# Idle waits of TensorE taken out, and steps around them reordered, in a fused attention kernel

## What is computed

```python
def _cross_attention(q_in, kv_in, wq, bq, wk, bk, wv, bv, wo, bo, bias_k, bias_v):
    qh = (q_in @ wq + bq).reshape(b, q_len, H, K)          # H = 16 heads, K = 128
    kh = (kv_in @ wk + bk).reshape(b, t, H, K)             # and one more key: bias_k
    vh = (kv_in @ wv + bv).reshape(b, t, H, K)             # and one more value: bias_v
    logits = jnp.einsum('bqhk,bthk->bhqt', qh, kh) / scale
    weights = jax.nn.softmax(logits, axis=-1)
    ctx = jnp.einsum('bhqt,bthk->bqhk', weights, vh).reshape(b, q_len, H * K)
    return ctx @ wo + bo
x = x + _cross_attention(_layer_norm(x, ...), ctx_2048, ...)   # first attention
x = x + _cross_attention(_layer_norm(x, ...), ctx_2048, ...)   # second attention
x = x + gelu(_layer_norm(x, ...) @ w_fc1 + b_fc1) @ w_fc2 + b_fc2
```

## Time and profile before

| | |
|---|---|
| median of 3 runs | 1567.48 us (1567.3 to 1568.53) |
| profiled execution | 1566.88 us |
| its span, first to last instruction | 1565.1 us |
| PE busy | 96% of the span |
| DVE, ACT, POOL busy | 62%, 56%, 27% |
| granted clock of TensorE | 0.997 on average |
| first block, to the end of the second's scores | 0 to 72.8 us |
| turn and block after | 455.5 to 538.9 us |
| last four steps | 867 to 922 us |

### The profile page before, as it was taken

One profiled execution on the slowest core, in us unless ns is written; L12 is line 12 of the kernel. 1 busy time (PEld: TensorE's weight loads), 2 busy tenths in 40 slices (PEclk: granted clock), 3 DMA queues, 4 the chain that ended last, 5 costly groups with the idle time before them and its releaser, 6 DMA issues. The chain is left out here.

```text
span 1565.1 us, 41346 instructions
## 1 busy us (share of the span) xinstructions
PE 1500.6 (96%) x17264; PEld 1301.6 (83%) x17264; DVE 970.8 (62%) x2122; ACT 874.0 (56%) x1638; POOL 419.4 (27%) x449
## 2 busy tenths in 40 slices
PE   4999999999999799999999999999999999999996
PEld 4788888888897688888888888988878988888864
DVE  4765646555467655564656676479996658865366
ACT  3835354363455453454453366577777567775476
POOL 1431020220201510210210123036774206542052
PEclk9999999999999999999999999999999999999998
DMA  5101010010010010010010000020002000001001
GB/s 173 42 29 42 1 68 2 28 43 1 28 42 1 28 42 2 28 43 1 29 42 29 28 2 28 1 83 3 3 29 82 1 16 15 30 2 28 8 22 54
DMA packets 17832, 46.20 MB, mean 30 GB/s; under 512 B 1360, under 2 KB 11616, under 8 KB 14704
## 3 DMA queue, kind: packets, MB, share of 16 engines
q1 hardware_dynamic: 13456, 39.33, 7.3%
q10 hardware_dynamic: 4192, 4.24, 0.8%
HBM read 39.37 MB, written 4.19 MB: 28 GB/s over the span
## 5 line engine op out<-in xcount | busy, mean ns | idle before, releaser
L174 PE MATMUL ps<-ch,W 128*128 128x512 f32 (+1 forms) x2484 | 579.4, 383 | 2.5 <-DVE ch L602 1.2
L174 PEld LDWEIGHTS ps<-ch,W 128*128 128x128 f32 x2484 | 435.6, 188 | 86.9 <-issue 3.8
L174 PEld LDWEIGHTS ps<-W,split_arena 128*128 128x128 f32 x3084 | 388.4, 188 | 23.1 <-issue 4.8
L174 PE MATMUL ps<-W,split_arena 128*128 128x256 f32 x3084 | 401.9, 283 | 3.1 <-DVE split_arena L1726 2.3
L1221 ACT ACTIVATE arena<-ps,hbias 128x512 f32<-128x512 f32 x128 | 87.8, 689 | 213.1 <-PE ps L174 195.2
L174 PE MATMUL ps<-W,ch 128*128 128x512 f32 (+1 forms) x864 | 195.2, 382 | 6.0 <-issue 3.8
L1383 DVE TENSOR_REDUCE small<-ps 128x4 f32<-128x260 f32 x128 | 53.7, 420 | 233.9 <-PE ps L773 233.6
L1206 ACT ACTIVATE arena<-ps 64x256 f32<-64x256 f32 x256 | 97.0, 379 | 170.1 <-PE ps L861 166.3
L174 PEld LDWEIGHTS ps<-W,ch 128*128 128x128 f32 x864 | 154.2, 188 | 38.8 <-issue 6.9
L1726 DVE TENSOR_TENSOR split_arena<-arena,split_arena 128x512 fp32r<-128x512 f32 x96 | 71.8, 748 | 125.4 <-ACT split_arena L1758 115.6
L1410 DVE TENSOR_TENSOR x_sb<-ps,x_sb 128x512 f32<-128x512 f32 x128 | 86.4, 688 | 93.7 <-PE ps L174 93.7
(11 more groups left out here) (173 smaller groups left out, 2036.3 us busy)
## 6 DMA issues: line engine op xcount, KB each, us to landing
raw<-wpack SPq DMA_DIRECT2D x23, 1028.0 KB, 4.8
rows<-vb_in SPq DMA_DIRECT2D x8, 512.0 KB, 5.7
x_sb<-x_in SPq DMA_DIRECT2D x4, 512.0 KB, 9.5
arena<-ctxT SPq DMA_DIRECT2D x4, 512.0 KB, 9.9
spill<-x_sb ACTq DMA_DIRECT2D x1, 2048.0 KB, 11.7
arena<-spill ACTq DMA_DIRECT2D x1, 2048.0 KB, 8.5
arena<-ctx_tok SPq DMA_DIRECT2D x16, 128.0 KB, 2.1
out<-x_sb SPq DMA_DIRECT2D x7, 256.0 KB, 2.5
```

What stands on the lines that cost most here:

```text
L174: last = e.matmul(dst, lhs[a], rhs[b], start=start and n == 0, stop=stop and n == 2, skip_group_check=True)
```

## The change

1. `idle` and its calls are gone (326 waits at the start, 6 x 60 after the turn); the 16 warm-up products stay.
2. `pe_values` and `pe_key` get `cut_at`: a step of the contraction that is named there issues its three products as six with half the columns. It is used for V products and some keys in the opening (27 steps), at the turn (16) and after it (14).
3. Pack 1: `second_act` (three copies on ACT) becomes `second_high` on DVE, ahead of each `second_dve`.
4. POOL in the opening: `context_lo(2)` waits for `second_mean`; the four `pool_row` stand behind the low half of chunk 3 and pack 1. At the turn: the `pool_row` of a chunk pair stand behind the low half of its second chunk.
5. DVE: `dve_lo` is ahead of `dve_mean(2)` in the opening, and ahead of the last V eviction of b at the turn. PE: transposes and queries of the second block alternate; at the turn `pe_query(a, 0)` is ahead of the second norm, and `norm_out(1, 1)` ahead of the queries of b.
6. Last pair (steps 60 and 61): heads of 58 go to bank 2 and keys of 61 to bank 6, the heads no longer wait for the queries' eviction, and ACT does both `act_probs` ahead of `act_queries`.

The diff, cut to the changed lines and their neighbours:

```diff
--- before.py
+++ after.py
@@ -289,11 +289,12 @@
-        def second_act(e, k):
+        def second_high(e, k):
...
             e.wait_ge(s_raw, 16)
-            e.activation(W[1][0][:, a], raw[:, a], ACT.Copy).then_inc(f_hi.sem, 1)
+            e.wait_ge(f_hi.sem, f_hi.at(len(FIRST) + k - 1))
+            e.tensor_copy(W[1][0][:, a], raw[:, a]).then_inc(f_hi.sem, 1)
@@ -682,7 +683,7 @@
         def keys_bank(t):
-            return {SINGLE: 4, SINGLE + 1: 2, SINGLE + 2: 0, SINGLE + 3: 0}[t] if t >= SINGLE else (4, 6)[t % 2]
+            return {SINGLE: 4, SINGLE + 1: 6, SINGLE + 2: 0, SINGLE + 3: 0}[t] if t >= SINGLE else (4, 6)[t % 2]
@@ -697,6 +698,8 @@
                 return (0, 4)[t % 2]
+            if t == SINGLE - 2:
+                return 2
             return 6 if t >= SINGLE else (6, 0)[t % 2]
@@ -774,18 +777,23 @@
-        def pe_project(e, t, k, off, src, bank, h):
+        def pe_project(e, t, k, off, src, bank, h, cut_at=()):
             c, w = t % NCH, W[t // NCH % 2]
             a = off + k * D + h * DH0
+            if k in cut_at:
+                for half in (0, CH // 2):
+                    last = split3(e, ps[:, bank, half:half + CH // 2], [x[:, a:a + DH0] for x in w],
+                                  [x[:, k, c * CH + half:c * CH + half + CH // 2] for x in src], k == 0 and half == 0, k == KT - 1)
+                return last
             return split3(e, ps[:, bank, :], [x[:, a:a + DH0] for x in w],
...
-        def pe_key(e, u, h):
+        def pe_key(e, u, h, cut_at=()):
...
             for k in range(KT):
-                ins = pe_project(e, u, k, 2 * D, cT, keys_bank(u) + h, h)
+                ins = pe_project(e, u, k, 2 * D, cT, keys_bank(u) + h, h, cut_at)
             ins.then_inc(a_k, 1)
@@ -829,7 +837,9 @@
-        def pe_values(e, t, i):
+        HALVES = (1, 0)
+
+        def pe_values(e, t, i, cut_at=()):
@@ -837,8 +847,12 @@
                     pack_ready(e, t, 1 + nth)
-                ins = split3(e, ps[:, values_banks(t)[i], :], [x[:, k, a:a + P] for x in cT],
-                             [x[:, 6 * D:8 * D] for x in W[1 - k]], nth == 0, nth == 1)
+                dst, lhs, rhs = ps[:, values_banks(t)[i], :], [x[:, k, a:a + P] for x in cT], [x[:, 6 * D:8 * D] for x in W[1 - k]]
+                if k in cut_at:
+                    for half in (slice(0, D), slice(D, 2 * D)):
+                        ins = split3(e, dst[:, half], lhs, [x[:, half] for x in rhs], nth == 0 and half.start == 0, nth == 1)
+                else:
+                    ins = split3(e, dst, lhs, rhs, nth == 0, nth == 1)
             ins.then_inc(a_V, 1)
@@ -957,21 +971,21 @@
             for i in range(TPC):
-                pe_values(e, 0, i)
+                pe_values(e, 0, i, HALVES)
             for h in range(2):
...
                 e.wait_ge(a_qe, two(0, h))
-                pe_key(e, 1, h)
+                pe_key(e, 1, h, HALVES)
             norm_out(e, 0, 0)
             for i in range(2):
-                pe_values(e, 1, i)
+                pe_values(e, 1, i, HALVES)
             e.wait_ge(a_ve, values_done(0, TPC - 1))
...
                 e.wait_ge(a_ke, two(0, i))
-                pe_values(e, 1, 2 + i)
+                pe_values(e, 1, 2 + i, HALVES)
             norm_out(e, 0, 1)
@@ -986,15 +1000,14 @@
                 e.wait_ge(a_sub, two(0, h))
-                pe_key(e, 2, h)
+                pe_key(e, 2, h, HALVES)
             norm_out(e, 0, 2)
             for h in range(2):
-                pe_key(e, 3, h)
+                pe_key(e, 3, h, HALVES[h:])
             pe_norm(e, 0, 3)
-            for i in range(2):
-                e.wait_ge(a_ke, two(2, i))
-                pe_transpose(e, i)
             for h in range(2):
+                e.wait_ge(a_ke, two(2, h))
+                pe_transpose(e, h)
                 e.wait_ge(a_ke, two(3, h))
@@ -1004,43 +1017,37 @@
-        PAGE_START, PAGE_TURN = 163, 30
-
-        def idle(e, n):
-
-            for _ in range(2 * n):
-                e.wait_ge(none_ok, 1)
-
         def pe_block_turn(e):
...
                 e.wait_ge(a_ke, two(b, i))
-                pe_values(e, a, i)
+                pe_values(e, a, i, HALVES)
             e.wait_ge(a_acc, two(a - 4, 1))
             for i in range(2):
-                pe_values(e, a, 2 + i)
+                pe_values(e, a, 2 + i, HALVES)
             e.wait_ge(a_pt, two(b - 2, 1))
...
             for i in range(2):
-                pe_values(e, b, i)
+                pe_values(e, b, i, HALVES)
             norm_out(e, 1, 0)
             for i in range(2):
-                pe_values(e, b, 2 + i)
+                pe_values(e, b, 2 + i, HALVES)
+            e.wait_ge(a_ve, values_done(a, 0))
+            pe_query(e, a, 0)
             e.wait_ge(a_ve, values_done(b, 1))
             pe_norm(e, 1, 1)
-            for h in range(2):
-                e.wait_ge(a_ve, values_done(a, h))
-                pe_query(e, a, h)
+            e.wait_ge(a_ve, values_done(a, 1))
+            pe_query(e, a, 1)
+            norm_out(e, 1, 1)
             for h in range(2):
...
             pe_heads(e, a - 2)
-            norm_out(e, 1, 1)
             pe_heads(e, b - 2)
@@ -1053,12 +1060,10 @@
                 e.wait_ge(a_ke, two(b, i))
-                pe_values(e, a, i)
-                idle(e, PAGE_TURN)
+                pe_values(e, a, i, HALVES)
             e.wait_ge(a_acc, two(a - 4, 1))
             for i in range(2):
-                pe_values(e, a, 2 + i)
-                idle(e, PAGE_TURN)
+                pe_values(e, a, 2 + i, HALVES)
             e.wait_ge(a_pt, two(b - 2, 1))
@@ -1067,13 +1072,12 @@
                 e.wait_ge(a_ve, values_done(a, i))
-                pe_values(e, b, i)
-                idle(e, PAGE_TURN)
+                pe_values(e, b, i, HALVES)
             e.wait_ge(a_ve, values_done(a, TPC - 1))
...
             for i in range(2):
-                pe_values(e, b, 2 + i)
+                pe_values(e, b, 2 + i, HALVES[:1])
             for h in range(2):
@@ -1101,32 +1105,31 @@
                 pe_query(e, t, h)
-            e.wait_ge(a_qe, two(t, 1))
+            e.wait_ge(a_acc, two(t - 4, 1))
             e.wait_ge(a_pt, two(t - 2, 1))
...
             pe_heads(e, t - 1)
+            e.wait_ge(a_qe, two(t, 1))
             e.wait_ge(a_kb, t // NCH + 1)
...
             for h in range(2):
-                e.wait_ge(a_acc, two(t - 5, h))
                 pe_key(e, t, h)
...
             pe_out(e, t - 3)
+            e.wait_ge(a_ke, two(t, 1))
             e.wait_ge(a_ol, two(t - 2, 1))
             pe_out(e, t - 2)
-            e.wait_ge(a_ke, two(t, 0))
             pe_transpose(e, t - 1)
...
             pe_heads(e, t - 1)
-            e.wait_ge(a_ke, two(t, 1))
             pe_scores(e, t)
@@ -1162,7 +1165,6 @@
         def pe_attend(e):
-            idle(e, PAGE_START)
             e.wait_ge(none_ok, 1)
@@ -1291,9 +1293,6 @@
             act_queries(e, 3)
-            for k in range(F_PIECES - 1):
-                second_act(e, k)
-
             for d in range(2, SINGLE // 2):
@@ -1322,8 +1321,8 @@
             act_probs(e, SINGLE - 2)
+            act_probs(e, SINGLE - 1)
             act_queries(e, SINGLE)
-            act_probs(e, SINGLE - 1)
@@ -1487,8 +1486,8 @@
             dve_mean(e, 1, 1)
+            norm0.dve_lo(e, 0, 1)
             dve_values(e, b, (1,))
-            norm0.dve_lo(e, 0, 1)
             dve_values(e, a, (2, 3))
@@ -1537,8 +1536,8 @@
             dve_values(e, 1, (0,))
+            norm0.dve_lo(e, 1)
             dve_mean(e, 0, 2)
-            norm0.dve_lo(e, 1)
             dve_values(e, 1, (1, 2, 3))
@@ -1550,6 +1549,7 @@
             for k in range(F_PIECES - 1):
+                second_high(e, k)
                 second_dve(e, k)
@@ -1613,6 +1613,7 @@
             e.wait_ge(c_lo.sem, c_lo.at(KT + KT - 1))
+            e.wait_ge(second_mean, 1)
             context_lo(e, 2)
@@ -1620,8 +1621,9 @@
             e.wait_ge(s_rows, 16)
+            norm0.split(e, NCH - 1)
+            e.wait_ge(w_lo.sem, w_lo.at(1))
             for c in range(NCH):
-                e.wait_ge(a_nrm, max(c, 1))
                 norm0.pool_row(e, c, row("bo1"))
@@ -1631,6 +1633,7 @@
                 norm0.pool_pow(e, c + 1, 1)
+                norm0.split(e, c + 1, 1)
                 norm0.pool_row(e, c, row("bo2"), 1)
...
```

## The result

| | before | after |
|---|---|---|
| median | 1568.01 us (4 runs, 1567.3 to 1568.68) | 1547.49 us (4 runs, 1546.73 to 1547.88) |
| profiled execution | 1566.88 | 1547.88 |
| its span | 1565.1 | 1546.1 |
| granted clock of TensorE, mean | 0.997 | 0.994 |

The time is inside the predicted range and 4.2 us above the predicted value. I went through PE's timeline of both kernels step by step and took the difference of the starts of equal rows.

The account below looks back on a forecast made before the run. TensorE bounds the kernel, busy 1500.6 of 1565.1 us. Opening 16.7, turn 1.4, after the turn 3.9 and last pair 1.6 sum to 23.6, so 1566.9 becomes 1543.3 us; range 1537.5 to 1549.

Parts of the forecast that it names:

- the views: Traces expected: first warm-up product near 2.3 us, keys near 8, second block's heads near 52, about 5 us wait on split.
- the likeliest case: The forecast itself: 1543.3 us, chance 0.42.
- Start and 54 ns per wait: Opening: without the waits at 54 ns each, warm-up starts near 2.3 us and first keys come 17.3 us earlier.
- ACT sets the opening: Opening: ACT's chain sets the pace, so heads start near 52.4, 16.3 us earlier; opening in all 16.7 us.
- paid out of that wait: Opening: PE's savings of 2 to 3 us become a wait for ACT, which covers the 81 divided products.
- Turn and last pair: Turn: 2.0 us kept of a 3.0 us wait, less 0.6 for division, 1.4; last pair: waits removed, 1.6 us.
- After the turn: Six groups of waits go, 9.2 us, but a new wait for weight pack 9 arises: gain 3.9 us.
- the pack wait: Second scores after the turn: PE waits 5.3 us (bounds 4.9 to 7.2) for POOL to split weight pack 9.
- Clock: Behind the wait for pack 9: nothing taken, bounds 0 to 2.3 us; as a rival 2.3 more, 1545.6, chance 0.22.
- Rival 6: Whole kernel: moved instruction stream exposes refills in heads and scores; slower, 1584 us at 0.3 us each; chance 0.04.
- Rivals 4 and 5: Opening: 4, loads land late, 1547 to 1550, chance 0.14; 5, late start isn't the waits, 1560.0, chance 0.05.
- Rival 3: After the turn: weight pack 9 isn't waited for, 5.3 us less, 1538.0 us; chance 0.13.

Follow-up runs that it names:

- the experiment with the rows early: Changed kernel with POOL adding the rows of a chunk pair at the turn ahead of the second chunk's low half, as before; 1541.42 us.
- the experiment with the last pair: Changed kernel with the last pair's banks, waits and order of ACT as they were before; 1548.31 us.
- the filled wait: Changed kernel with 28 unread identity products (56 records) added on PE ahead of the awaited weight pack 9; 1549.06 us.
- no halves: Changed kernel with no product divided, the waits still gone; 1557.14 us.

## Why the prediction came out as it did

The sign, the range and the views were right; the likeliest case was not. From 1543.3 to the measured 1547.9 of the profiled execution: +2.05 after the turn, +2.4 clock, +0.65 small steps not foreseen, +0.1 last pair, -0.6 opening.

- **Start and 54 ns per wait: right.** The first product began at 2.28 as said. The first keys were at 8.72, not 7.95, because the warm-up took 6.44 us, not 5.4; it varied between 5.2 and 6.7 us among kernels whose start is the same. ACT's chain absorbs that: in the kernel with the last pair as before the first keys start 0.85 us sooner, and at the end of the opening 0.14 is left. One window of the warm-up, of the changed kernel and then of the kernel before without waits (columns as above), shows where the length comes from:

```profile
6.00:7.00 1.00, 1.00 (x7) 1.00 (x6) 0.69 (x6) 0.31 (x1) 0.00 (x0) 1.00 0.97 274
...
6.00:7.00 1.00, 1.00 (x12) 1.00 (x11) 0.82 (x7) 1.00 (x2) 0.00 (x0) 1.00 0.94 244
```

  The same records pass at 6 or 7 a microsecond and later at 11 or 12, and the moment of the change differs: not before 8 us in the one, near 5 in the other. In the kernel before too, the last records of the warm-up are faster (11 in the microsecond from 23.84, 5 to 7 ahead of it). That looks like the two clock levels, although the clock column reads 1.00 all the while; so the prediction's remark that the granted clock "reads 1.00 in both" was no evidence against a low clock at the start.
- **ACT sets the opening: right in the main.** Heads at 51.84 (forecast 52.4), chunk 2 normalised on ACT from 31.9 to 33.9 (forecast 32.1 to 34.2), and the reordering alone worth 0.6 to 0.95 us. The term was 16.7 and measured 17.3, of which the waits alone give 16.7 (the kernel before without them). But the divided products were not "paid out of that wait": without them the heads start at 50.69 and the opening ends 1.0 us sooner. And the copies didn't hold the heads in the kernel before, as I had read the earlier trace rows; they do only in the new one.
- **Turn and last pair: right**, 1.4 and 1.5 for 1.4 and 1.6. The first is all due to POOL's rows, as the experiment with the rows early shows, the second was shown by the experiment with the last pair.
- **After the turn: mechanism right, term mis-sized,** 3.9 forecast, 1.85 measured. The norm came at the forecast place (499.91, or 518.4 in the frame of before, which is 18.5 us later there). The step that failed is the end of DVE's low half of chunk 3 "at about 523.0". It was 525.1. I had let ACT evict chunk 3 as soon as PE had transposed it, but `act_norm` and `dve_lo` share one buffer, so ACT's eviction waits 2.30 us for DVE's low half of chunk 2. From the norm's start to the end of the low half it is 6.7 us, where the sum had 4.6. POOL's rows and the split took 11.1 us against 11.7 assumed, which gave 0.5 back. The last score records at the low clock, 0.6 us for the 0.3 of the sum, took the rest. Without the pack wait the stretch is shorter by 9.0 us (24.2 for 33.2), close to the 9.2 that the prediction had.
- **Clock: wrong end taken.** The pack wait was priced at 0 with 0 to 2.3 as bounds, "nearer" to the 3.0 us gap. What came was just above the upper bound: 2.4 us, shown by the filled wait. The row it rested on was itself a poor support, since an equal gap of 3.02 us in another kernel was followed by the low clock. The Trainium skill (TensorE: Matmul & The Clock Gate, Part 1) had the direction right, that the clock falls with idling.
- **Rival 6 was dismissed by a false argument.** "No such gap in some 30 blocks at changing positions": the positions don't change freely. In the kernels with a row of gaps these recur every 55 or 110 us, all but a few at the same record, until an edit or the turn moves them. So the 30 blocks are not 30 trials, and the kernel before happened to have none. The removed waits did move the stream, by enough to cost some 8 us of gaps (no halves, before without waits); the divided products, which I priced by their 13 ns alone, moved it back. The price was there too: up to 1.8 us per gap, 12.8 us in sum. That the forecast time held in spite of this was luck: the change brings its own counterweight. The Trainium skill (Runtime: NRT & Kernel Launch, Instruction fetch mechanics) calls crossing a block mostly hidden; for most of the 137 pieces here that holds, for many that fall into the scores it doesn't.
- **Rivals 4 and 5** did not happen: the first product is at 2.28, and the longest wait of ACT for a load between 8 and 30 us is 0.90.
- **Rival 3** (pack not waited for, 1538.0) did not happen, but its number is what the kernel gives once POOL's order is mended: 1537.5.

Still open: the rule that gives the place of a gap ahead of time, what sets the moment at which the pace of the warm-up changes, and the 0.65 us of small steps.

## What to carry to other kernels

When an engine's work is moved behind a later event, follow that event back through every shared buffer to the engine that really ends last, and ask which queue item stands behind the moved work: some 10 us, half as much as this change won, were lost to a weight split behind eight cheap additions, and moving the split won them back. Before removing or adding instructions of PE, look where its instruction pieces fall: in dense small products a refill may not be covered, and an edit far away can open a gap in every repetition, so judge an edit by the rows without a releaser as well as by its own stretch. Price a new idle time of TensorE of several microseconds with the low clock behind it.

## What the runs showed of the hardware

- At gaps in the scores, PE goes on 2.2 to 2.9 us after the transfer of an instruction piece of 16 KB begins. Behind nearly 1 MB of weights the piece began 1.0 us ahead of PE's stop (126.85), with the queues empty 2.0 us ahead (182.06).
- The clock level after an idle time isn't a matter of its length alone: 3.00 us left it at 1.00 in one kernel, 3.02 was followed by 0.59 and 0.56 in another, and 4.5 and 6.9 us by 0.50. It cost 1.45 to 2.4 us each time.
- The warm-up products pass at 6 or 7 records a microsecond and, from a moment that differs between kernels with the same start, at 11 or 12; the profile's clock column reads 1.00 throughout.
- Two of DVE's operations on 128x4 elements rose from 0.16 to 1.24 us, and one to 0.64, beside the first subtractions of POOL's split; its 128x256 operations out of PSUM stayed at 0.41 to 0.42 us beside a later one.
